# Value products in blocks of eight steps instead of four, with eighteen buffers of probabilities instead of ten

## The reference

```
L0: xn = rms(x)*gq; k, v from rms(ctx)*gkv; q from xn;  x = xn + softmax(q k^T / sqrt 8) v Wo + bo
L1: q from x; k, v from ctx (a mask, here all false);   x = layernorm(x + softmax(...) v Wo + bo)
L2: causal attention of x over the first 100 rows of ctx, then layernorm, then a gelu MLP of width 512, plus the residual
L3: q from x; k, v from ctx;                            x = layernorm(x + softmax(...) v)
```

## Time and profile before

| | before |
|---|---|
| runs, us | 1160.42, 1166.34, 1167.5 |
| median, us | 1166.34 |
| the profiled execution, us | 1159.32 |
| its span from first to last instruction, us | 1157.5 |
| mean granted TensorE clock | 0.950 of 2.4 GHz |
| TensorE matmuls, share of the span | 91% |
| VectorE | 70% |
| ScalarE | 66% |
| GpSimd | 25% |

### The profile page before, as it was taken

How to read it: one execution, slowest core, us unless ns; L and a number is a source line. 1 busy time by engine, 2 the same in 40 slices (tenths; PEclk the granted TensorE clock), 3 DMA queues, 4 the chain that set the end, 5 groups by cost and what they waited for, 6 DMA issues and landing times.

```text
span 1157.5 us, 24776 instructions
## 1 busy us (share of the span) xinstructions
PE 1054.8 (91%) x9410; PEld 597.1 (52%) x9410; DVE 812.2 (70%) x1681; ACT 761.9 (66%) x1692; POOL 292.2 (25%) x267
## 2 busy tenths in 40 slices
PE   2689999999899999999999999999989999999996
PEld 1345555555455555555555555555555555564542
DVE  5787778768657767777876667676767777766851
ACT  1266776677577776867774666666666666756676
POOL 5644333532121122012113040404040313221100
PEclk9779999999999999999998899989899989998999
DMA  7421321221222222222231211112120202121100
GB/s 201 107 73 53 85 74 51 66 78 44 80 65 76 72 78 67 76 70 81 77 84 43 66 40 56 45 50 65 31 74 24 80 18 80 34 63 52 29 4 4
DMA packets 64350, 72.81 MB, mean 63 GB/s; under 512 B 8187, under 2 KB 59899, under 8 KB 64104
## 3 DMA queue, kind: packets, MB, share of 16 engines
q1 hardware_dynamic: 64232, 71.22, 21.6%
HBM read 50.25 MB, written 18.15 MB: 59 GB/s over the span
## 4 chain that ended last, share of the span: by engine, by line
PE 68%; DVE 16%; ACT 8%; issue 4%; SPq 1%; POOL 1%; DMA 0%; ACTq 0%; POOLq 0%; DVEq 0%
PE acc L709 17%; PE ring L650 15%; PE sexp L689 15%; PE ring L596 5%; PE ring L588 4%; DVE mx L1081 4%; DVE mneg L1087 4%; DVE mx L1079 3%; PE ring L622 2%; ACT probs L957 2%; PE ring L624 2%; PE ring L773 2%; ACT kp L903 2%; SPq L457 1%; PE ring L577 1%
## 5 line engine op out<-in xcount | busy, mean ns | idle before, releaser
L1081 DVE TENSOR_TENSOR mx<-ring,mx 120x400 f16<-120x400 f32 (+1 forms) x1056 | 556.2, 568 | 220.6 <-PE ring L650 217.3
L957 ACT ACTIVATE probs<-sexp 120x400 f32<-120x400 f32 (+1 forms) x1152 | 540.7, 514 | 191.5 <-PE sexp L689 186.6
L650 PE MATMUL ring<-qx,krep 96*128 96x400 f16 (+2 forms) x1152 | 399.1, 351 | 38.6 <-ACT kp L903 14.2
L689 PE MATMUL sexp<-qx,krep 97*128 97x400 f16 (+2 forms) x1152 | 396.3, 348 | 8.2 <-ACT probs L957 4.5
L709 PE MATMUL acc<-probs,vx 120*18 120x200 f32 (+1 forms) x4608 | 262.6, 347 | 0.8 <-ACT probs L957 0.7
L689 PEld LDWEIGHTS sexp<-qx,krep 97*128 97x128 f16 (+2 forms) x1152 | 126.3, 111 | 150.0 <-ACT probs L957 84.8
L650 PEld LDWEIGHTS ring<-qx,krep 96*128 96x128 f16 (+2 forms) x1152 | 128.5, 112 | 133.9 <-DVE mx L1081 31.0
L476 POOL TENSOR_TENSOR kp<-kf,kp 128x480 f16<-128x480 f32 (+1 forms) x72 | 80.9, 1130 | 357.3 <-ACT kp L903 357.3
L709 PEld LDWEIGHTS acc<-probs,vx 120*18 120x18 f32 (+1 forms) x4608 | 108.7, 99 | 118.6 <-issue 84.1
L503 POOL TENSOR_TENSOR qx<-qs,headmask 96x400 f16<-96x400 f16 x96 | 79.9, 862 | 78.7 <-DVE qs L1068 44.0
L914 ACT COPY vx<-ring 120x512 f32<-120x512 f32 (+1 forms) x72 | 42.3, 587 | 68.2 <-PE ring L596 68.2
(11 more groups left out here) (123 smaller groups left out, 924.3 us busy)
## 6 DMA issues: line engine op xcount, KB each, us to landing
krep<-kept SPq DMA_DIRECT2D x144, 120.0 KB, 2.6
ctf<-in_ctxT SPq DMA_DIRECT2D x16, 722.0 KB
kept<-kp SPq DMA_DIRECT2D x48, 240.0 KB, 2.8
krep<-kept SPq DMA_DIRECT2D x72, 121.0 KB, 2.8
kept<-kp SPq DMA_DIRECT2D x24, 242.0 KB, 2.5
nat<-in_ctx SPq DMA_DIRECT2D x8, 720.0 KB
maskexp<-maskmax SPq DMA_DIRECT2D x8, 281.2 KB, 3.4
anymask<-in_mask SPq DMA_DIRECT2D x1, 1128.1 KB, 6.8
```

The source lines that it names most:

```text
L650: last = pe.matmul(ps[0:n, 0:QW], krep[0:PARTS, u.par, t, c0:c0 + n], qx[0:PARTS, u.third, t, :, :].rearrange("p f s -> p (f s)"), start=T ...
L689: last = pe.matmul(ps[0:n, 0:QW], krep[:, u.par, t, c0:c0 + n], qx[:, u.third, t, :, :].rearrange("p f s -> p (f s)"), start=True, stop=no ...
L957: act.activation(probs[0:r, j % PR, :], sexp[j % SR][0:r, 0:QW], ACT.Exp).then_inc(sem["probs_ready"], 1)
L1081: op = dve.tensor_tensor(dst, src, dst, ALU.max)
```

## The change

`TOGETHER` becomes 8. The products of steps 0 to 7 are issued at step 10, those of 8 to 15 at step 18, then at 26, 34 and 42, and those of steps 40 to 47 at step 2 of the next stage: six blocks of sixteen products (32 records) for a unit instead of twelve of eight (16 records). The blocks at steps 6, 14, 22, 30, 38 and 46 are gone, and those at 2, 10, 18, 26, 34 and 42 have twice the length. `probs` has 18 buffers of 400 f32 columns instead of 10, since the first product of a block is now issued ten steps after its exponential. The arithmetic is the same.

```
--- before.py
+++ after.py
@@ -44,7 +44,7 @@
 MASKED = [-30000.0, -1e30]
 VW = 2 * (DH + 1)
 PAIRS = H // 2
-PR, SR, RING = 10, 3, 4
+PR, SR, RING = 18, 3, 4
 PARTS = 96
 
 
@@ -69,7 +69,7 @@
        "pt2": 34, "pt3": 36, "o": 40, "scale": 45}
 AT2_FF = {"at": 1, "h": 8, "w2": 13}
 
-TOGETHER = 4
+TOGETHER = 8
 VALUES_AT = [j // TOGETHER * TOGETHER + TOGETHER + SR - 1 for j in range(NSTEP)]
 LEAD = 13
 ACC_AT = 3
```

## The result

The change made the kernel slower: 1201.96 us, the median of 4 runs (1199.09 to 1203.52), against 1163.8 us of 4 runs of the kernel before (1160.42 to 1167.5). The ratio is 1.032, with an interval of 1.030 to 1.035. The sign is the forecast's; the size, +38, is nearly three times the +14 of the forecast and outside its range. In the profile the span went from 1157.5 to 1201.7 us, +44.2. Medians and ratios in this document leave out the executions that took over 1.5% more than the fastest of the same kernel; there were four, one of join38to42 (1456.48 us) and three of joins_by_stage (1166.12 to 1171.02 us, one of them the profiled one).

A forecast was written before the change was run, and what follows sets the result against it. TensorE was taken to bound most of each stage, chains on ScalarE or VectorE the rest. Stage sums of 0.8 + 5.1 + 7.6 + 0.5 = +14 us gave 1180 us as a median, range 1150 to 1196.

The forecast's parts named there:

- What bounds, and what the change saves: TensorE bounds most of a stage; 144 fewer blocks at 0.23 us of end cost save 33 us of its work.
- Rival one: The saving on TensorE is kept, making the kernel faster: 1133 us if all, 1150 if half; chance 0.16.
- rival two: It comes out even because small waits at steps 6, 14 and 30 don't grow: near 1166 us; within 1%, chance 0.32.
- Rival three: Slower still, by the clock or by waits of twice the size: 1190 to 1196 us; chance 0.12.
- Where it is given back: Per stage, removed blocks count -0.90 us and lengthened ones +0.67 on TensorE's path, 0 inside waits; sum +14 us.
- Step 14: Removed block, partly given back as a wait: -0.60 us in the first five stages, -0.55 in the nine before layer 2.
- Step 22: Removed block on TensorE's path in the stages without layer 2, counted in full at -0.90 us.
- Steps 26, 30 and 34 in the nine stages before layer 2: Removing 30 gives -0.60 us after a wait of some 0.3; lengthening 26 and 34 costs +0.67 each.
- Step 38 with layer 2, Step 46 with layer 2: Removed block in the eight layer-2 stages, taken as on TensorE's path: -0.90 us a stage.
- hidden by VectorE's chain: First five stages: VectorE works without a gap, so removing 30 and 38 gives nothing and lengthening 34 costs nothing.
- The clock: I take 0: Longer waits at steps 41 and 42 can add stretches at 1.2 GHz; counted as 0, up to +10 us.

The follow-up runs named there:

- join38to42: Kernel before with eighteen buffers, the block of step 38 issued with that of step 42 in every stage; 1159.20 us, ratio 0.998 to the kernel before.
- joins_by_stage: Kernel before, eighteen buffers, 26 joined to 30 except in the nine stages before layer 2, 38 to 42 with layer 2; 1152.13 us, ratio 0.991.
- eights_keys_at_once: Changed kernel (blocks of eight steps) with ScalarE reading both parts of a group's keys in the same step; 1177.54 us, ratio 1.012 to the kernel before.
- eights_keys_v0_later: Changed kernel with both key parts read at once and the first value projection at step 23 instead of 22; 1184.44 us, ratio 1.018 to the kernel before.
- join38to42_layer2: Kernel before with eighteen buffers, block of step 38 joined to that of 42 only in the eight layer-2 stages; 1154.74 us, ratio 0.993.
- join26to30: Kernel before with eighteen buffers, the block of step 26 issued with that of step 30 in every stage; 1152.14 us, ratio 0.991.
- buf18: Kernel before with only the buffers of probabilities raised from ten to eighteen, blocks still of four steps; 1162.57 us, ratio 0.999.
- twos: Kernel before with eighteen buffers and blocks of two steps, four products each; 1243.21 us, ratio 1.067 to the kernel before.

## Why the forecast had the sign and not the size

**What bounds, and what the change saves: right.** The block of sixteen costs 1.58 us, the end cost is 0.23 at each length, and TensorE's share fell three points. The busy time did not show the 33 us less. Rival one, the saving kept, is out; so is rival two, that it comes out even. Rival three, slower still at 1190 to 1196 by waits of twice the size or by the clock, named the kind of cause, and still fell short.

**"Where it is given back": the step that failed.** Its method, a removed block counted at 0.90 or at 0 by what waits around it, holds for most lengthened blocks (+0.67 or +0.68) and for step 6 (-0.75 and -0.53 against -0.80 and -0.50). The terms for removed blocks were too favourable, because only the waits of the kernel before were read, and not those that the blocks kept from showing:
- Step 14, -0.60 and -0.55: measured -0.29 and -0.18. The wait of step 18 was expected to grow and did not, which the prediction had named as a sign that it is wrong; a new one came at step 15. Steps 14 to 15 are 0.96 shorter and 15 to 16 are 0.67 and 0.80 longer. Shown by eights_keys_at_once.
- Step 22, -0.90: measured -0.53 in the stages without layer 2 (all of the first five, one of the nine). The trace shows a new wait for VectorE's reading of the queries' bank there; moving the projection past it brought nothing, as eights_keys_v0_later showed.
- Steps 26, 30 and 34 in the nine stages before layer 2: removing 30, forecast at -0.60, gives 0.89 at once in eight of them, but lengthening 34 takes 1.06 and lengthening 26 takes 1.08, in place of 0.67 each. 23 to 35 is +1.34 against +0.74.
- Step 38 with layer 2, -0.90: worth nothing. join38to42_layer2 has it so at full clock in one stage and as the mean of eight.
- Step 46 with layer 2, -0.90: in five stages most of it comes back at the next step 1 (+0.82 in the unit shown). This is read from the trace and was not tried alone.

In the fourteen stages without layer 2 the stretches at full clock add up to 5 x 1.1 + 9 x 2.1 = 25 us, against 0.8 + 5.1 in the forecast: 19 us of waits that were not counted, where the forecast missed by 24 in all. (As executed they add up to 14.8, since the nine spent less time at 1.2 GHz than before.) With layer 2 the blocks of steps 14 and 22 gave nothing in sum, as forecast: of the 0.81 of step 14 (1.48 - 0.67, the 0.67 being what the wait of step 12 takes in of the block of step 10), 0.76 come back at 16 to 19, and in five stages 22 to 23 is 1.00 shorter and 23 to 27 is 1.68 longer, 1.0 more than its lengthened block.

In the first five stages steps 30, 34 and 38 were called hidden by VectorE's chain. The sum held: +0.15 + 0.46 = +0.61 over steps 27 to 43, forecast +0.67. The reason did not: removing 30 gives 0.89 at once, and lengthening 34 takes 1.04.

**"The clock: I take 0": open.** As executed, the stages of L0 and L1 are 4.2 and 4.7 us above their forecast sums, those with layer 2 19.6 us. In this pair of executions the time at 1.2 GHz rose by 34 us in the stages with layer 2 and fell by 14 in the nine before them. At half speed the 34 are worth up to 17 us, if TensorE is the bound throughout, which the trace does not tell stretch by stretch; the prediction allowed +10. Over whole kernels the time at 1.2 GHz is nearly the same, 127 and 130 us as means, so its sum does not explain the 38 us. How much of the 19.6 is due to the clock, to step 1, to step 38 and to the longer wait of step 30 stays open, since the clock could not be held fixed.

**Other parts: right.** The buffers cost nothing.

## What to carry to other kernels

A block of work on the busiest engine that stands just before a wait for a buffer is also that buffer's time to come free: before removing it, look not only at the waits that the trace shows but at every use of the ring behind it, and work out how late its last reader ends. Join or move such blocks one at a time and by kind of stage; here the six joins together cost 3.2%, while one of them alone gained 0.9% (1.1 us of it by its stretches; the rest goes with less time at 1.2 GHz) and one with an earlier read of the keys 2.0%. A sum by stretches between fixed instructions, kernel against kernel, shows in one table which join pays in waits. Before the clock is given as a cause, look at it in several executions of each kernel: two single profiles here suggested 19 us more at 1.2 GHz, and the means differ by 3.

## What the runs showed beyond that

- Stretches that ran without a spell at 1.2 GHz repeat between kernels to some nanoseconds: join26to30 against buf18 differs by about 0.002 us or less in eleven of thirteen stretches of the first five stages. Within one kernel the time at 1.2 GHz accounts for 82% of the variance between executions.
- With the same products in the same number, by their placing alone, the time at 1.2 GHz went from 100 us (88 to 114, join38to42) to 202 us (193 to 206, twos). The first costs 9 us by its stretches without layer 2, and its median is still 3.4 us below buf18's.
- A block's two ends cost 0.23 us at 8, 16 and 32 records, among f16 products at a pitch of 0.17 us (means at full clock).
